# Reciprocal head sums spread in one fp16 pass, both ends of the run rearranged, and a new order of steps in an eight-image attention and expert kernel

## The reference, cut to what matters

```python
def attention(x):                                  # x = _ln_c(x)
    qkv = einsum('bcxy,oc->boxy', x, w_qkv) + b_qkv   # 3 x (4 heads x 32)
    q = softmax(q, axis=-2) * scale                # over the 32 channels of a head
    k = softmax(k, axis=-1)                        # over the 4096 positions
    context = einsum('bhdn,bhen->bhde', k, v / n)
    out = einsum('bhde,bhdn->bhen', context, q)
    out = einsum('bcxy,oc->boxy', out, w_out) + b_out
    return (out - mean) * rsqrt(var + eps) * g_ln  # over channels
x = x + attention(_ln_c(x))
t = tokens(x)                                      # 4096 tokens of 32
p = softmax(_ln_t(t) @ router_w + router_b)        # 8 experts
top_p, top_i = top_k(p, 2); top_p /= sum(top_p)
out = t + sum_k top_p[k] * (_ln_t(t) @ expert_w[top_i[k]] + expert_b[top_i[k]])
```

## Time and profile before

| | before |
|---|---|
| median of 3 runs | 405.4 us (405.0 to 409.66) |
| profiled execution, own time | 406.5 us |
| its span | 404.6 us |
| PE busy | 314.1 us (78%) |
| PE weight loads busy | 186.3 us (46%) |
| DVE busy | 288.1 us (71%) |
| ACT busy | 231.4 us (57%) |
| POOL busy | 215.2 us (53%) |
| granted TensorE clock, mean | 0.93 |

### The profile page before, as it was taken

One profiled execution on the slowest core, in us unless ns is written; L12 is line 12 of the kernel. 1 busy time (PEld: TensorE's weight loads), 2 busy tenths in 40 slices (PEclk: granted clock), 3 DMA queues, 4 the chain that ended last, 5 costly groups with the idle time before them and its releaser, 6 DMA issues.

```text
span 404.6 us, 7765 instructions
## 1 busy us (share of the span) xinstructions
PE 314.1 (78%) x2896; PEld 186.3 (46%) x2896; DVE 288.1 (71%) x383; ACT 231.4 (57%) x409; POOL 215.2 (53%) x245
## 2 busy tenths in 40 slices
PE   0452779877899999999999999899989888745460
PEld 0342545244446644664475457435734563234240
DVE  3416653753988889898989898988798869336670
ACT  1230186688678757966786678657756765620100
POOL 8401101460298458835883588359717951874560
PEclk9865699999999999999999999999999999978595
DMA  2635011014202311340233013301421120111101
GB/s 69 125 104 134 3 40 41 2 59 98 54 5 80 93 35 47 104 97 16 65 100 92 13 49 78 81 12 41 93 67 25 48 60 2 51 40 42 29 23 52
DMA packets 14236, 22.97 MB, mean 57 GB/s; under 512 B 5334, under 2 KB 5368, under 8 KB 14200
## 3 DMA queue, kind: packets, MB, share of 16 engines
q1 hardware_dynamic: 13864, 22.47, 22.1%
q10 hardware_dynamic: 336, 0.02, 0.0%
HBM read 4.38 MB, written 4.19 MB: 21 GB/s over the span
## 4 chain that ended last, share of the span: by engine, by line
PE 44%; DVE 11%; SPq 10%; POOL 10%; ACT 8%; issue 7%; DMA 6%; POOLq 0%; ACTq 0%; PEldq 0%; DVEq 0%
PE narrow L934 23%; PE wide L934 10%; SPq L355 8%; PE small L934 6%; PE sums L937 4%; POOL xhat L518 4%; DVE kmax L815 3%; DMA stack<-high 3%; DMA x_in<-in_x_dram 3%; POOL low L523 2%; ACT eq L601 1%; ACT high L584 1%; DVE gated L887 1%; POOL scaled L508 1%; ACT high L640 1%
## 5 line engine op out<-in xcount | busy, mean ns | idle before, releaser
L887 DVE TENSOR_TENSOR gated<-wide,gates 128x1024 f32<-128x1024 f32 x64 | 76.6, 1219 | 23.2 <-PE wide L934 21.2
L503 POOL TENSOR_TENSOR paired<-gated 128x512 f32<-128x512 f32 x64 | 81.5, 1284 | 17.0 <-PE sums L937 12.1
L934 PE MATMUL wide<-w_stack,stack 128*128 128x256 f16 (+1 forms) x512 | 58.0, 256 | 7.5 <-DVE gated L887 5.2
L934 PEld LDWEIGHTS wide<-w_stack,stack 128*128 128x128 f16 x512 | 40.7, 101 | 36.1 <-issue 16.2
L479 POOL TENSOR_TENSOR xhat<-centered,rstd 128x992 f32<-128x992 f32 x8 | 15.0, 1877 | 70.3 <-PE small L934 46.5
L815 DVE TENSOR_REDUCE kmax<-wide 128x1 f32<-128x1024 f32 x32 | 39.0, 1222 | 15.2 <-PE wide L934 14.4
L590 ACT ACTIVATE ek<-narrow,wscale 128x512 f32<-128x512 f32 x64 | 41.2, 685 | 10.9 <-PE narrow L934 8.0
L937 PE MATMUL sums<-ident,paired 128*128 128x128 f32 x256 | 39.6, 289 | 9.5 <-POOL paired L503 8.3
L601 ACT ACTIVATE eq<-narrow,wscale 128x512 f32<-128x512 f32 x64 | 42.3, 688 | 7.7 <-PE narrow L934 6.6
L811 DVE TENSOR_TENSOR eq<-eq,wide 128x1024 f32<-128x1024 f32 x32 | 38.7, 1212 | 7.3 <-PE wide L934 7.3
L804 DVE TENSOR_REDUCE nqmax<-wide 128x32 f32<-128x1024 f32 x32 | 38.3, 1219 | 5.7 <-PE wide L934 4.6
(11 more groups left out here) (146 smaller groups left out, 574.5 us busy)
## 6 DMA issues: line engine op xcount, KB each, us to landing
stack<-high SPq DMA_DIRECT2D x128, 64.0 KB, 2.0
x_in<-in_x_dram SPq DMA_DIRECT2D x8, 512.0 KB
stack<-low SPq DMA_DIRECT2D x64, 64.0 KB, 2.0
out_dram<-y_out SPq DMA_DIRECT2D x8, 512.0 KB
stack<-ones SPq DMA_DIRECT2D x5, 256.0 KB, 7.8
w_rows<-in_L_ffn_expert_w_dram SPq DMA_DIRECT2D x3, 32.0 KB
g_col<-in_L_conv_g_ln_dram ACTq DMA_DIRECT2D x4, 0.1 KB
w_nat<-in_L_conv_w_qkv_dram SPq DMA_DIRECT2D x1, 48.0 KB, 3.7
```

The lines of the kernel that those rows point to most:

```text
L503: nc.gpsimd.tensor_tensor(paired[:, n % PAIREDS, :, :, :], gated[:, n % GATEDS, 0:E // 2, :, :], gated[:, n % GATEDS, E // 2:E, :, :], ALU ...
L887: nc.vector.tensor_tensor(gated[:, n % GATEDS, :, :, :].rearrange("p e t c -> p t e c"), src.rearrange("p (t e c) -> p t e c", t=4, e=E), ...
L934: return nc.tensor.matmul(dst, lhs, rhs, start=start, stop=stop)
```

## The change

1. **The spread in fp16.** `headcols` now holds 1/32, so `z` gives the mean of a head's exponentials, and `headrows` (now fp16) also holds 1/32. After Ln and Exp a third ACT operation, `zhigh`, rounds the reciprocal to fp16 in the rows where `is_low` is one (rows 16 to 31 of each 32) and gives zero in the others. A new POOL step, `zlow` (`reciprocal_parts`), subtracts: `zparts` holds the fp16 high part of the reciprocal in rows 0 to 15 and the low part in rows 16 to 31. One fp16 contraction over the 32 rows adds both. `bc` waits for `zparts`.
2. **100 rows for 128.** Products with the stacks contract over rows 0 to 99; the ones fill writes four rows (32 KB) and not 32, and is started by ACT.
3. **Start.** The first image is loaded in two halves, one from SP and one from ACT. `set_up_operands` and the weight maxima stand first on DVE, and PE's `set_up_maxima` directly behind the transposes. The diagonal matmul stands behind `xc` of image 0. For image 0 ACT starts the DMAs of quarters 1 and 3 of `stack1`.
4. **Fills.** The high parts of a quarter are sent before the wait for the low part. For the last image ACT starts the DMAs of quarters 1 and 3 of `stack3`.
5. **Stores.** y is stored by halves (256 KB); the last half in two pieces, from SP and ACT.
6. **Order.** Every number of `AT` is new, and so is the order on every engine.

```diff
-SETUP_V = 38
-PERIOD, STEPS = 2113, range(45496)
+SETUP_V = 39
+ROWS = 100
+PERIOD, STEPS = 1368, range(24699)
...
-    "z": (16389, 17067),
-    "bc": (16717, 16737, 17120, 17123),
+    "z": (4652, 4722),
+    "bc": (4795, 4831, 5130, 5130),
...
+    "zlow": (12370, 12384),
...
-SETUP = {'transposes': 10766, 'maxima': 13490, 'operands': 19378, 'scales': 20577, 'act': 20541}
+SETUP = {'transposes': 1126, 'diagonal': 3130, 'operands': 0, 'scales': 6704, 'act': 9044}
...
-        headrows = sb("headrows", [P, HEADS, DH])
+        headrows = sb("headrows", [P, HEADS, DH], f16)
...
+        zhigh = sb("zhigh", [P, R, RT], f16)
+        zparts = sb("zparts", [P, R, RT], f16)
+        is_low = sb("is_low", [P, 1])
...
-        ws_q = w_stack[:, 0:CH]
-        ws_k = w_stack[:, CH:2 * CH]
-        ws_e = w_stack[:, 2 * CH:2 * CH + E * C]
-        ws_r = w_stack[:, 2 * CH + E * C:NW]
+        ws_q = w_stack[0:ROWS, 0:CH]
+        ws_k = w_stack[0:ROWS, CH:2 * CH]
+        ws_e = w_stack[0:ROWS, 2 * CH:2 * CH + E * C]
+        ws_r = w_stack[0:ROWS, 2 * CH + E * C:NW]
...
-            load(0)
+            sp.dma_start(x_in[:, 0, 0:RT], x_0[:, :, :, 0:RT].rearrange("b j c i -> (b j) c i")).then_inc(x_first, 16)
...
+            def fill_quarter(k, b, j, stack, ready):
+                cols = slice(N // J * j, N // J * j + N // J)
+                for rows in (0, 2 * C):
+                    sp.dma_start(stack[rows:rows + C, cols], high[k][C * j:C * j + C, :]).then_inc(ready, 16)
+                if k == 1:
+                    sp.wait_ge(wide_free, wide_turn["xc", b, 0] + 1)
+                else:
+                    sp.wait_ge(low3_ready, nth("low3", b, R - 1) + 1)
+                sp.dma_start(stack[C:2 * C, cols], low[k][C * j:C * j + C, :]).then_inc(ready, 16)
...
+            for n in range(2 * J):
                 nc.gpsimd.affine_select(out=headrows[:], in_=headrows[:], pattern=[[-1, HEADS], [0, DH]],
-                                        compare_op=ALU.not_equal, fill=1.0, base=-C * j,
+                                        compare_op=ALU.not_equal, fill=1.0 / DH, base=-C // 2 * n,
                                         channel_multiplier=1).then_inc(made, 1)
-                pool.wait_ge(made, 21 + j)
+                pool.wait_ge(made, 21 + n)
...
+            def reciprocal_parts(b, r):
+                pool.wait_ge(zhigh_ready, nth("z", b, r) + 1)
+                if b > 0:
+                    pool.wait_ge(wide_full, wide_turn["bc", b - 1, 2 * r + 1] + 1)
+                nc.gpsimd.tensor_tensor(zparts[:, r, :], zrec[:, r, :], zhigh[:, r, :],
+                                        ALU.subtract).then_inc(zparts_ready, 1)
...
+            nc.scalar.dma_start(x_in[:, 0, RT:], x_v[bass.ds(0, 1)][:, :, :, RT:].rearrange("b j c i -> (b j) c i")).then_inc(x_loaded[0], 16)
+
+            def fill_ones(stack):
+                nc.scalar.dma_start(stack[96:ROWS, :].rearrange("c (j i) -> c j i", j=J),
+                                    ones16[96:ROWS, :].unsqueeze(1).broadcast_to([ROWS - 96, J, N // J])).then_inc(ones_copied, 16)
+
+            def fill_odd_quarters(k, stack, ready):
+                for j in (1, 3):
+                    for rows, part in ((0, high[k]), (2 * C, high[k]), (C, low[k])):
+                        nc.scalar.dma_start(stack[rows:rows + C, N // J * j:N // J * j + N // J],
+                                            part[C * j:C * j + C, :]).then_inc(ready[j], 16)
...
+            act.wait_ge(ones_made, 1)
+            for k in range(STACKS):
+                fill_ones(stack1[:, k, :])
+            for k in range(2):
+                fill_ones(stack3[:, k, :])
...
+                if b == 0:
+                    act.wait_ge(high1_ready, 1)
+                    act.wait_ge(wide_free, at + 1)
+                    fill_odd_quarters(1, stack1[:, 0, :], stack1_ready[0])
...
+                    act.wait_ge(zparts_ready, nth("zlow", b - 1, r) + 1)
                 nc.scalar.activation(zrec[:, r, :], src, ACT.Ln).then_inc(narrow_free, 1)
                 act.wait_ge(narrow_free, at + 1)
                 nc.scalar.activation(zrec[:, r, :], zrec[:, r, :], ACT.Exp, scale=-1.0).then_inc(zrec_ready, 1)
+                act.wait_ge(zrec_ready, nth("z", b, r) + 1)
+                nc.scalar.activation(zhigh[:, r, :], zrec[:, r, :], ACT.Copy, scale=is_low[:, 0:1]).then_inc(zhigh_ready, 1)
...
+                if b == NB - 1 and r == R - 1:
+                    act.wait_ge(high3_ready, nth("high3", b, r) + 1)
+                    act.wait_ge(low3_ready, nth("low3", b, r) + 1)
+                    fill_odd_quarters(3, stack3[:, b % 2, :], stack3_ready[b % 2])
...
+            act.wait_ge(y_ready, nth("y", NB - 1, R - 1) + 1)
+            nc.scalar.dma_start(out_v[bass.ds(NB - 1, 1)][:, 2:J, :, RT:].rearrange("b j c i -> (b j) c i"),
+                                y_out[P // 2:P, RT:]).then_inc(stored[1], 16)
...
-                st.inc(nc.vector.tensor_copy(headcols[:], headmask[:, :, 0].unsqueeze(1).broadcast_to([P, 8, HEADS])))
+                st.inc(nc.vector.tensor_scalar(headcols[:], headmask[:, :, 0].unsqueeze(1).broadcast_to([P, 8, HEADS]),
+                                               1.0 / DH, None, ALU.mult))
...
+                st.inc(nc.vector.tensor_reduce(is_low[:], ident[:].rearrange("p (j a h) -> p j a h", j=J, a=2)[:, :, 1, :],
+                                               AX.XY, ALU.add))
...
                     set_up_operands()
+                    set_up_maxima()
...
+            def set_up_diagonal():
+                pe.wait_ge(setup_v, 30)
                 mm(sums[:, 256:259], ones[0:3, :], gdiag[:, :]).then_inc(setup_t, 1)
+
+            def set_up_done():
...
+                if b == 0 and u == 0:
+                    pe.wait_ge(x_first, 16)
...
-                    pe.wait_ge(zrec_ready, nth("z", b, r) + 1)
+                    pe.wait_ge(zparts_ready, nth("zlow", b, r) + 1)
...
-                             headrows[rows, :, :].rearrange("p h d -> p (h d)"), zrec[rows, r, :])
+                             headrows[rows, :, :].rearrange("p h d -> p (h d)"), zparts[rows, r, :])
```

213 lines of the change are left out of this document (107 added, 106 removed).

## The result

The changed kernel took 419.39 us (median of four, 416.65 to 422.53) against 405.2 for the kernel before, a ratio of 1.033 (95% interval 1.0225 to 1.0433). The profiled execution took 416.65, 10.15 more than the 406.5 against which the forecast's sum was made. Here are the same views of the changed kernel.

A forecast was written before the change was run, and what follows sets the result against it. The prediction took PE to set the pace. Spread 6.1, start 6.3, last fill 3.7 and last store 3.3 summed to 19.4 us off the profiled 406.5: 387.1, or 386 as a median, range 376 to 399.

The forecast's parts named there:

- The middle's term: Spread on PE between first and last `attend`: fp16 matmuls save 0.87 us per image, 6.1 us over seven.
- The new order opens holes: Rival: DVE's `ws_kmax`, ahead of the fourth `gated`, waits for PE; 3 us per image, 21 in all, 407; chance 0.08.
- the sequence of stages is kept: Argument against the rival "The new order opens holes": the new order leaves the stages in sequence; no size given.
- So PE sets the pace: Middle: PE, busy 36.59 of 38.90 us per image, is the bound, with DVE only 2.1 us behind.
- the saving passes to the period: Middle: PE stays busiest (35.7 against DVE's 34.49), so 0.87 us per image shortens the period, 6.1 us in all.
- Their idle time holds both: Spread's added operations: ACT (to 30.0 of 38 us per image) and POOL (to 27.8) absorb them in idle time.
- POOL's new link gives the middle back: Rival: one 1.16 us POOL operation per image falls on the path, costing 8.1 us, 394; chance 0.20.
- The start: Filling of the pipeline: earlier set-up and image 1 landing at 19.5 gain 6.3 us, bounds 2.5 and 9.8.
- Last store: End: the last y store, 256 KB from two queues, gains 3.3 us, bounds 0 and 4.5.
- Last fill: End: the last `stack3` fill, issued from ACT and SP, gains 3.7 us, bounds 0 and 3.8.
- the landings and not the issues decide: Lower bound of the last `stack3` fill's gain: 0 us if DMA landings set its end.
- The 100 rows: Stack products on PE: matmuls and weight loads over 100 rows for 128 were given no change in time.

The follow-up runs named there:

- e1: The changed kernel with the load of x put back ahead of `fill3` and the two stores in SP's queue: 400.16 us.
- e4: The changed kernel with the kernel before's order of steps and fp32 spread, so only the new code of the two ends is left: 393.39 us.
- e14: e4 with ACT's Exp writing fp16 reciprocals directly, spread by fp16 matmuls without high and low parts: ratio 0.980 to the kernel before.
- e3: e1 with the fp32 spread of the kernel before, without the high and low parts: 409.94 us.
- e13: e5 with the high and low parts computed but not used; PE spreads fp32 reciprocals with fp32 matmuls: 409.3 us.
- e5: The changed kernel with the kernel before's order of steps, high and low parts kept: 413.58 us.
- e15: e14 in the order of steps of e1 (fp16 reciprocals straight from ACT's Exp, no parts): 396.38 us.
- e7: e1 with the two `z` groups set one and two `kexp` groups later and the first two `bc` groups behind them: 431.2 us.
- e12: e4 with the last fill of the last image's stack on SP's queue alone, as before: 395.09 us.

## Why the prediction was wrong, by its own steps

**A moved step was not costed.** The middle's term was 7 x 0.87 less, "This assumes that the new order leaves as many holes as the old one". The order moved the load of x behind `fill3` and two stores in SP's queue, and no term, bound or rival spoke of it. e1 prices it: 18.0 us of span, all of it between the first and the last `attend` (19.8). My rival "The new order opens holes" had nearly the size by which the middle missed (21 us for 22.1), but another place (`ws_kmax`) and a chance of 0.08; that it came near is luck. Against it I held that "the sequence of stages is kept". In SP's queue it was not.

**"So PE sets the pace" failed, and with it "the saving passes to the period".** I took the busiest engine for the bound. The fp16 groups were even cheaper than sized: a step of two takes 0.32, and a step of four 0.33 (e1, below) where I had 0.57, 0.98 an image for 1.27. A group of two takes 0.1 us more than a lone matmul of 0.22. (The Trainium skill, "TensorEngine Tiling (Array Packing)", Key Properties, has the rule that a change of tiling mode drains the engine; that the 0.1 is this drain is not shown.) Yet from e4 to e14 only this changed, and nothing was gained.

```profile
218.67 0.40 PE L988 MATMUL wide<-zparts,headrows 32*128 32x512 f16 x4 [0.33 <-PE small L988]
219.00 0.65 PE L991 MATMUL sums<-ident,paired 128*128 128x128 f32 x4
```

In the order before, the period hung on a path through three engines: logits on ACT, `route` and `mixb` on DVE, `attend` on PE. DVE, 2.1 us behind in busy time, was on it. The profile of before already had a sign of it. Two of its neighbouring stretches, the first with the centring of a later image on PE (2.2 us of matmuls), the second without:

```profile
186.16:225.10 38.94, 36.63 (x366) 21.84 (x362) 34.46 (x44) 28.77 (x52) 25.46 (x27) 1.00 0.26 69
225.10:263.85 38.75, 35.48 (x348) 20.32 (x346) 34.45 (x44) 28.17 (x52) 25.48 (x27) 1.00 0.23 56
```

PE has 1.15 us less to do and the period is 0.19 shorter. The new order does the same in e1: its periods with centring are 38.0, those without 37.9 and 37.8, and in the latter PE stands 1.6 us ahead of `attend`, which starts 0.1 behind `mixb`. But there the spread as a whole gained 9.8 (e3 against e1), more than the 6.1: the new order with the fp32 spread is 11.9 us longer in its seven periods than the order before (278.3 for 266.4), and the fp16 spread brings most of that back.

**"Their idle time holds both" failed in the order before.** ACT's 0.72 had room in the period but not where it stood, ahead of the logits. The rival "POOL's new link gives the middle back" named the right neighbours (`xhat`, `route`) and 8.1 us. In the order before it was 16 to 20, by the medians (e13, e5). The new order avoids it: in e1 `gap` takes 0.19 and `tie` 0.42, clear of `xhat`, the parts cost 7.2 in all (e15), and with z set later again it loses some 30 more (e7). Why the fp32 spread costs 11.1 us of span there, when its groups are only 1.16 us an image longer (8.1 in seven), was not tried.

**The start was right, the end was not.** That e4's 13.0 is near the forecast 13.3 is in part luck: 9.9 lies at the ends, 3.0 in the middle. Start: 6.3 forecast, 7.2 in e4, and `nqmax` at 39.32 in the changed kernel (forecast 38.5); image 1 landed at 21.5, not 19.5, inside the bounds (its transfer took 9.1 instead of 12.35, but was issued at 12.43 instead of 10.06, which I had not allowed for). The new order then gave back 4.4 of the 7.2, in e1 5.2: 2.2 with the parts (e1 against e15), of which I had allowed 1.5, and 3.0 with its other steps (e15 against e4), which I had at nothing. Last store: SP's last wait, which answers to the earlier trace rows, fell by 1.9 of the 3.3:

```profile
SPq L400 <- DMA out_dram<-y_out: 7.6, 1, 7.6
```

Last fill: 3.7 forecast, nothing by e12. In the changed kernel itself router still waited for it. From the end of `low3` (372.48) to router (382.22) is 9.7 us where it was 10.4:

```profile
371.32 1.16 POOL low L535
...
375.88 6.10 DMA stack<-low
...
382.22 1.01 PE small L988 x32
```

The last issue is 3.4 us behind the end of `low3`, where I had 3.8 for the six, but the landing takes 6.10 instead of 3.38. That was my lower bound ("the landings and not the issues decide").

**The 100 rows** cost nothing: router's 32 loads and products took 1.01 for 0.97.

Sum against the profile: start -2.8, middle +16.0, rest -2.9 is +10.3. Without the late load, e1: -2.0, -3.8, -1.9, 7.7 of the forecast 19.4. The rest went to the new order at the start (4.3), to the end (5.1) and to the middle (2.3).

## What to carry to other kernels

When a table of steps moves, list every queue with what each issue now stands behind, and compare the time from issue to first use with that of before: the x load went from 24 us ahead of its use to 9, and that outweighed all the rest. Before a cheaper operation is credited to the busiest engine, follow the chain that releases its next step: saved time on PE is worth nothing, or less, when another engine's short operation releases it. And undo order and operation separately, in all four pairs, since here the same spread was worth +20 us or -10 us.
